# Counting the edges of a graph network beside two of its edge sums, in place of a stage of their own

## What is computed

```python
# layer 0: a small network on every edge, summed at its target
out = segment_sum(leaky(norm(leaky(norm([x[src], x[dst]] @ w1)) @ w2)) * edge_weight, dst)
# layer 1, twice: mean over the incoming edges
mean = segment_sum(h[src], dst) / maximum(segment_sum(1, dst), 1)
# layer 2, twice: the edges and a loop at each node, scaled by the root of the count on both sides
deg  = segment_sum(1, dst) + 1
out  = segment_sum((x @ W)[src] / sqrt(deg[src] * deg[dst]), dst) + b
# layer 3: softmax over the edges that leave a node, then a weighted sum at dst
```

## Time and profile before

| | us |
|---|---|
| median of 3 runs | 8127.6 |
| lowest and highest | 8127.11, 8133.38 |
| the profiled execution | 8135.82 |
| its span, first to last instruction | 8134.1 |

### The profile page before, as it was taken

How to read it: one execution, slowest core, us unless ns; L and a number is a source line. 1 busy time by engine, 2 the same in 40 slices (tenths; PEclk the granted TensorE clock), 3 DMA queues, 4 the chain that set the end, 5 groups by cost and what they waited for, 6 DMA issues and landing times. The chain is left out here.

```text
span 8134.1 us, 136717 instructions
## 1 busy us (share of the span) xinstructions
PE 5193.6 (64%) x26951; PEld 4126.4 (51%) x26952; DVE 4104.8 (50%) x13878; ACT 2865.5 (35%) x7066; POOL 4035.8 (50%) x4542
## 2 busy tenths in 40 slices
PE   4446766666037696669767857666666666605667
PEld 1125555555036585558656646544444444404555
DVE  8965555533522321236523422386566666653568
ACT  0015555523623431258524313573111111100249
POOL 0037777500057504770277167504777777707740
PEclk7767777788556897589857966897777777755689
DMA  0002222255633484349646745674222222232458
GB/s 3 0 23 72 73 73 73 68 177 195 203 102 101 138 247 135 93 124 312 227 116 189 244 124 152 194 259 139 65 68 68 68 65 68 64 25 69 105 164 298
DMA packets 616678, 1013.31 MB, mean 125 GB/s; under 512 B 174962, under 2 KB 177296, under 8 KB 616336
## 3 DMA queue, kind: packets, MB, share of 16 engines
q1 hardware_dynamic: 279472, 417.77, 17.6%
q10 hardware_dynamic: 211680, 385.45, 13.3%
q0 software_dynamic: 125440, 209.18, 10.9%
HBM read 648.88 MB, written 363.07 MB: 124 GB/s over the span
## 5 line engine op out<-in xcount | busy, mean ns | idle before, releaser
L397 PE MATMUL agg_bank<-agg_msgs,agg_onehot 128*128 x7840 | 1620.5, 374 | 894.0 <-DVE agg_onehot L372 695.9
L397 PEld LDWEIGHTS agg_bank<-agg_msgs,agg_onehot 128*128 128x128 f32 x7840 | 1403.7, 268 | 1114.1 <-issue 1104.6
L372 DVE TENSOR_TENSOR agg_onehot<-iota,rel 128x512 f32<-128x512 f32 x1176 | 814.3, 692 | 1819.4 <-PE agg_bank L397 856.5
L303 POOL DMA_INDIRECT agg_msgs<-y,agg_rows x784 | 776.6, 991 | 234.8 <-issue 189.9
L291 POOL COPY agg_rows<-src_row_of 128x16 int32 (+2 forms) x100 | 23.5, 235 | 1623.4 <-POOLq L59 1623.1
L397 PE MATMUL agg_bank<-agg_weighted,agg_onehot 128*128 x1568 | 339.9, 387 | 217.1 <-DVE agg_onehot L372 168.6
L1090 POOL DMA_INDIRECT mlp_xs<-in_x,mlp_rows x392 | 412.4, 1052 | 120.1 <-issue 119.2
L300 POOL DMA_INDIRECT agg_weight<-weights,agg_rows x392 | 409.7, 1045 | 123.3 <-issue 99.6
L424 ACT ACTIVATE agg_kept<-agg_bank,inv_root 128x128 f32<-128x128 f32 x784 | 224.1, 368 | 700.3 <-PE agg_bank L397 679.7
L424 ACT ACTIVATE agg_kept<-agg_bank,inv_deg 128x128 f32<-128x128 f32 x784 | 224.1, 368 | 695.4 <-PE agg_bank L397 694.7
L1422 PE MATMUL score_pSrc<-ident,score_xs 128*128 128x128 f32 x392 | 154.3, 401 | 485.2 <-issue 356.2
(11 more groups left out here) (338 smaller groups left out, 12993.9 us busy)
## 6 DMA issues: line engine op xcount, KB each, us to landing
sums<-agg_kept ACTq DMA_DIRECT2D x588, 256.0 KB
agg_first<-y ACTq DMA_DIRECT2D x196, 256.0 KB
messages<-mlp_m SPq DMA_DIRECT2D x98, 256.0 KB, 2.1
agg_first<-in_x ACTq DMA_DIRECT2D x98, 256.0 KB
agg_msgs<-messages SPq DMA_DIRECT2D x98, 256.0 KB
l_z<-sums SPq DMA_DIRECT2D x98, 256.0 KB
x<-l_o ACTq DMA_DIRECT2D x98, 256.0 KB
l1a_s<-sums SPq DMA_DIRECT2D x98, 256.0 KB
```

The lines of the kernel that those rows point to most:

```text
L303: pool.indirect_dma_start(msgs[:, j, :], None, table[:, :], bass.IndirectOffsetOnAxis(ap=rows[:, third, j:j + 1], axis=0)).then_inc(sm[f"g ...
L372: nc.vector.tensor_tensor(onehot[:, j, :, :], k.iota[:, 0:P].unsqueeze(1).to_broadcast([P, Q, P]), k.rel[:, ds(i * (4 * Q) + j * Q, Q)].un ...
L397: t.matmul(bank[:, column[q], :], onehot[:, j, q, :], messages[:, slot[q], :], start=False, stop=True, skip_group_check=True)\
```

## The change

The stage `count_nodes` is gone. The splits of `src` and `dst` into tile and place go to `setup`, for both. `aggregate` gets an argument `tally`. In `agg0` it holds the split of `dst`, in `agg3` that of `src`. There each round of four steps also takes two edge tiles: VectorE makes two pairs of hot rows behind `onehot`, TensorE does two matmuls into a bank of counts behind the reading of the places, with the semaphores `hot` and `tallied` between them and four buffers. 196 rounds of two tiles are the 392. What was worked out from the counts now stands at the end of these two sums. The other four sums are as before but for more names of semaphores to clear.

```diff
+                for to_lo, to_hi, node in ((k.src_lo, k.src_hi, k.src_i), (k.dst_lo, k.dst_hi, k.dst_i)):
+                    c.link(v.tensor_scalar(part_i[:, :], node[:, :], P - 1, None, ALU.bitwise_and))
+                    c.link(v.tensor_copy(to_lo[:, :], part_i[:, :]))
+                    c.link(v.tensor_scalar(part_i[:, :], node[:, :], 7, None, ALU.logical_shift_right))
+                    c.link(v.tensor_copy(to_hi[:, :], part_i[:, :]))
+                c.link(v.memset(k.zero_row[:, :], 0.0))
...
                             ALU.is_equal).then_inc(sm["onehot"], 1)
+                        if tally is not None:
+                            dve.wait_ge(sm["tallied"], i * 4 + (j + 1))
+                            for w in range(2):
+                                at = i * 8 + (j * 2 + w)
+                                nc.vector.tensor_scalar(hot_lo[:, j, w, :], k.iota[:, 0:P], tally[0][:, ds(at, 1)], None, ALU.is_equal)
+                                last = nc.vector.tensor_scalar(hot_hi[:, j, w, :], k.iota[:, 0:NT], tally[1][:, ds(at, 1)], None, ALU.is_equal)
+                            last.then_inc(sm["hot"], 1)
+
+                v, c = nc.vector, Chain(dve, sm["tally_c"])
+
+                def count_in():
+                    c.link(v.tensor_scalar(k.inv_deg[:, :], counts[:, 0:NT], 1.0, None, ALU.max))
+                    c.link(v.tensor_scalar(k.inv_root[:, :], counts[:, 0:NT], 1.0, None, ALU.add))
+                    dve.sem_inc(sm["tally_to_act"], 1)
+                    c.link(v.reciprocal(k.inv_deg[:, :], k.inv_deg[:, :]))
+                    dve.wait_ge(sm["tally_rooted"], 1)
+                    c.link(v.reciprocal(k.inv_root[:, :], k.root[:, :]))
...
+                if tally is not None:
+                    dve.wait_ge(sm["tallied"], STEPS // Q + 4)
+                    if tally[0] is k.dst_lo:
+                        count_in()
+                    else:
+                        count_out()
...
+                if tally is not None:
+                    t.matmul(counts[:, 0:NT], k.zero_row[0:1, 0:P], k.zero_row[0:1, :], start=True, stop=True)
+                    pe.sem_inc(sm["tallied"], 4)
                 pe.sem_inc(sm["summed"], SHIFT)
...
                             pe.reg_load(regs[half:half + Q], k.places[0:1, ds(i * 4 + (j + 1), 1), half:half + Q])
+                        if tally is not None:
+                            pe.wait_ge(sm["hot"], i * 4 + (j + 1))
+                            for w in range(2):
+                                last = t.matmul(counts[:, 0:NT], hot_lo[:, j, w, :], hot_hi[:, j, w, :], start=False, stop=True, skip_group_check=True)
+                            last.then_inc(sm["tallied"], 1)
+                if tally is not None and tally[0] is not k.dst_lo:
+                    pe.wait_ge(sm["tally_to_pe"], 1)
+                    t.matmul(off[:, 0:1], below[:, :], scan[:, NT - 1:NT], start=True, stop=True).then_inc(sm["tally_offset"], 1)
...
+                if tally is not None and tally[0] is k.dst_lo:
+                    act.wait_ge(sm["tally_to_act"], 1)
+                    a.activation(k.root[:, :], k.inv_root[:, :], ACT.Sqrt).then_inc(sm["tally_rooted"], 1)
...
-        count_nodes(nc, k)
...
-        aggregate(nc, k, "agg0", messages, None, sums, before=ins["x"])
+        aggregate(nc, k, "agg0", messages, None, sums, before=ins["x"], tally=(k.dst_lo, k.dst_hi))
...
-        aggregate(nc, k, "agg3", y2, k.src_row, sums, before=y2, scale=k.inv_root)
+        aggregate(nc, k, "agg3", y2, k.src_row, sums, before=y2, scale=k.inv_root, tally=(k.src_lo, k.src_hi))
```

More of the change, by code:

```diff
@@ L244, in setup, with aggregate @@
         end_phase(nc, sm)
-def aggregate(nc, k, name, table, rows_of_edges, out, before=None, scale=None, weights=None):
+def aggregate(nc, k, name, table, rows_of_edges, out, before=None, scale=None, tally=None, weights=None):
     BLOCKS, REST = ET // RING, ET % RING
@@ L257, in aggregate @@
     sm = phase(nc, name, [f"gathered{j}" for j in range(loads)] + [f"written{u}" for u in range(BANKS)] + [f"before{u}" for u in range(BANKS)]
-               + [f"weight{u}" for u in range(RING // Q)] + ["rows", "pass_pool", "pass_dve", "arrived", "onehot", "summed", "zeros", "cleared", "ready", "emptied", "weighted"])
+               + [f"weight{u}" for u in range(RING // Q)] + ["rows", "pass_pool", "pass_dve", "arrived", "hot", "tallied", "tally_c", "tally_to_act", "tally_rooted", "tally_to_pe", "tally_offset", "onehot", "summed", "zeros", "cleared", "ready", "emptied", "weighted"])
     with ExitStack() as ctx:
@@ L265, in aggregate @@
         kept = sb("kept", [P, BANKS, Q, C])
+        if tally is not None:
+            hot_lo, hot_hi = sb("hot_lo", [P, 4, 2, P], BF16), sb("hot_hi", [P, 4, 2, NT], BF16)
+            counts = ctx.enter_context(nc.psum_tensor(name + "_counts", [P, 512], F32))
+            scan, one_row, below, offset = sb("scan", [P, NT]), sb("one_row", [P, NT]), sb("below", [P, P]), sb("offset", [P, 1])
+            off = ctx.enter_context(nc.psum_tensor(name + "_off", [P, 512], F32))
         if rows_of_edges is not None:
@@ L376, in _, with count_out @@
                             ALU.is_equal).then_inc(sm["onehot"], 1)
+                        if tally is not None:
[13 more added lines that the diff above has]
+                    c.link(v.reciprocal(k.inv_root[:, :], k.root[:, :]))
+                def count_out():
+                    c.link(v.memset(one_row[:, :], 1.0))
+                    c.link(v.tensor_scalar(below[:, :], k.iota[:, 0:P], k.pid[:, 0:1], None, ALU.is_gt))
+                    c.link(v.tensor_tensor_scan(scan[:, :], one_row[:, :], counts[:, 0:NT], 0.0, ALU.mult, ALU.add))
+                    dve.sem_inc(sm["tally_to_pe"], 1)
+                    c.link(v.tensor_tensor(k.first_place[:, :], scan[:, :], counts[:, 0:NT], ALU.subtract))
+                    dve.wait_ge(sm["tally_offset"], 1)
+                    c.link(v.tensor_copy(offset[:, :], off[:, 0:1]))
+                    c.link(v.tensor_scalar(k.first_place[:, :], k.first_place[:, :], offset[:, 0:1], None, ALU.add))
+                if tally is not None:
[4 more added lines that the diff above has]
+                        count_out()
             @block.tensor
@@ L1767, in allocate @@
     k.src_hi = sb("src_hi", [P, ET])
+    k.dst_lo = sb("dst_lo", [P, ET])
+    k.dst_hi = sb("dst_hi", [P, ET])
+    k.zero_row = sb("zero_row", [1, NT], BF16)
     k.src_row = sb("src_row_of", [P, ET], I32)
```

79 lines of the change are left out of this document (removed).

## The result

| | before | changed |
|---|---|---|
| median of the runs shown together, us | 8128.98 (4 runs) | 7720.11 (4 runs) |
| lowest and highest | 8127.11, 8133.38 | 7718.73, 7721.56 |
| the profiled execution | 8135.82 | 7720.17 |
| mean granted clock | 0.74 | 0.76 |

The changed kernel takes 0.9497 of the time, 95% interval 0.9485 to 0.9509: 408.9 us less. The forecast was 7766, with 7710 to 7834 around it. The sign and the range held, but the likeliest value was 46 us too high, and 7720 lies 10 us from the first rival's 7710, near the low end of the range. So the question is which term of the sum went wrong.

What follows compares the result with a forecast made beforehand. Stages add up; TensorE's queue was taken to bound the first sum, POOL's gathers most of the fourth. -432.1 + 3.5 + 39 + 16 + 7 + 4.3 + 0.5 = -361.8 us, giving 7766 us, range 7710 to 7834.

Steps and rivals of the forecast that it cites:

- first rival: Both sums: clock stays fast and the new matmuls sit in TensorE's 0.7 us idle gap each round; 7710 us, 20% chance.
- Stage removed, setup longer: Counting stage and its barrier go, -432.1 us; eight conversions and a memset move into setup, +3.5 us.
- VectorE in the first sum: Two hot-row pairs add 1.06 us a round, 1.8 to 1.9 in all, under TensorE's 2.08: no cost.
- TensorE in the first sum: Point 4 of the prediction: one more wait and two matmuls a round lengthen the first sum by 39 us.
- With 62% of the time fast: First sum: old clock mix kept, rounds of 2.15 us fast and 2.54 slow give a mean of 2.28.
- One more wait: First sum: a further wait in TensorE's queue, read from the sixth sum, adds 0.11 us a round.
- TensorE in the fourth sum: Same addition to TensorE's rounds, but only the last 105 or so are near its limit: +16 us.
- POOL in the fourth sum: Gathers beside VectorE's new operations slow by 0.032 us each, 12.5 us, less 5 where TensorE is the limit: +7.
- Ends: After the last matmul, the work on the counts adds 4.3 us to the first sum and 0.5 to the fourth.
- The issue is dear: Both sums: each new matmul holds TensorE's queue 0.15 us, +80 for +39 and +43 for +16; 7834 us, 17% chance.
- POOL is locked out: Fourth sum: each of 392 gathers waits for a full hot-row pair, 0.53 us, +208 for +7; 7967 us, 4% chance.
- Lock-step: Both sums: VectorE and TensorE wait for each other, 4.3 us a round, +764; 8475 us, slower than before, 2% chance.

Runs made afterwards that it cites:

- e2: Changed kernel, but the first sum's hot rows are zeroed once and not made, its two matmuls a round kept: 8847.7 us, ratio 0.9529; first sum 410.6 us.
- e10: Changed kernel, unedited, rerun on another chip: 8860.1 us beside 9278.1 for the kernel before, ratio 0.9559; first sum 411.8 us, fourth 619.4.
- e5: Changed kernel, but both counts in the first sum (four hot-row pairs and matmuls a round), none in the fourth: 8958.0 us, ratio 0.9629; first sum 530.0 us.
- e1: Changed kernel, but the first sum's count matmuls left out, hot rows and waits kept: 8872.1 us, ratio 0.9548; first sum 431.8 us.
- e11: Repeat, on another chip, of the changed kernel without the first sum's count matmuls, hot rows and waits kept: 8848.1 us, ratio 0.9557; first sum 432.3 us.
- e12: Changed kernel, but the first sum has neither hot rows nor count matmuls, only the waits and increments: 8864.8 us, ratio 0.9567; first sum 430.4 us.
- e8: Changed kernel with the source count moved to the fifth sum; fourth sum does two matmuls a round on zeroed rows, no hot rows: 8856.2 us, fourth sum 605.9.
- e7: Changed kernel with the source count moved to the fifth sum; fourth sum makes hot rows without matmuls, waits kept: 8886.3 us, fourth sum 617.4.
- e6: Changed kernel, but outgoing edges counted beside the fifth sum, not the fourth: 8849.2 us, ratio 0.9523; fourth sum 601.7 us, fifth 617.9.
- e9: Kernel before the change, unedited, rerun on another chip: 9283.5 us, ratio 1.0; first sum 406.9 us, fourth 603.7.

## Why the prediction was right, and where it was not

1. **Stage removed, setup longer: right.** -428.3 for -428.6, and -427.4 on another chip.
2. **VectorE in the first sum: right.** 1.06 us a round and no cost while VectorE is ahead; e2 without the hot rows is within 1.2 us of e10, and e5 shows the 0.53 a pair at full load. The 1.8 to 1.9 that it took for VectorE's round was a little high, as e5's distances make it 0.6 + 2 x 0.53 = 1.66.
3. **TensorE in the first sum: wrong, and 34 of the 46 us.** Forecast +39, measured +4.7, which is the prediction's own sign of being wrong, a first sum within 10 us of its old length. Two steps of the prediction's fourth point failed.
   - "With 62% of the time fast" took the granted clock of before as given. The change itself set it: 3 slow rounds in place of 69, and with the matmuls a clock of 0.99 (e2, e10), without them 0.76 to 0.78 (e1, e11, e12), whatever VectorE does. The 2.54 us for a slow round was about right. The first sum has too few of them left to tell (2.42 for three, 2.73 for two in e10), but the slow rounds of the fourth sum, shown under e10, take 2.52 and 2.36 where they wait for nothing. With every round at the forecast's fast 2.15 the term would have been 196 x (2.15 - 2.08) = 14, so by this estimate 25 of the 34 us missed are the clock.
   - "One more wait", +0.11. It was read from the sixth sum, where no run separates it. e12 gives 0.11 to 0.12 for a wait and an increment together that have nothing to ride on. In the changed kernel they are part of the count's matmuls and cost nothing that can be seen. This is the other 9 us.
4. **TensorE in the fourth sum: wrong.** Forecast +16; e8, the matmuls without the hot rows, gives +4.2, and the ledger leaves nothing for it. From TensorE's starts the last 105 rounds took 225.9 us before and take 230.4, 4.5 more with POOL's part in them. The clock was taken as given here too: in these rounds it went from 0.82 to 0.99.
5. **POOL in the fourth sum: right in kind, and too small by the deduction.** 32 ns a gather was taken from the scatters of the scoring stage, and the gathers grew by 32 ns on the first chip: 12.5 us. That it is the same number is luck, since they grew by 22 ns in e10 and 14 in e7. I had let 5 of them go as hidden under TensorE's limit, and since TensorE didn't become the limit, they weren't.
6. **Ends: right.** +4.1 for +4.3, and -0.8 for +0.5.

The range held because it reached down to the first rival, not because the forecast's mechanism was right. *TensorE hides it* is what happened, and it deserved more than its 20%. What I held against it, that the clock fell before with the array just as busy, was an argument from a kernel without the matmuls. *The issue is dear* falls: four matmuls cost 1.9 us and eight 16.1, all of it array. *POOL is locked out* falls by the fourth sum's 12.2 us, and by e7. *Lock-step* falls: both sums together grew by 17 us and not by 764.

What stays open: why the array's clock went up. Shown is that it goes up with the matmuls and down without them; what of their activity matters was not separated. Nor do the runs tell why the standing semaphores cost 0.11 at the fast clock and 0.15 at the slow one. I found no version that beats the change: both counts in the first sum are slower (e5), and the fifth sum is no cheaper than the fourth (e6). The dense stages between the sums, which have no gathers, were not tried as a place; in each of them VectorE or TensorE is busy for over half of the time.

## What to carry to other kernels

Work for an engine that a queue bounds was nearly free here as long as its matmuls fitted into the gap and brought no standing wait or increment into that queue: let both ride on the work. Don't carry the granted clock of the old profile into the sum: added matmuls can set it, so work out a fast and a slow case and name which the change makes likelier. And a neighbour's price read from another stage of the same kernel, here 32 ns a gather, was of the right size, where the worst case, a wait for every pair, was some 200 us off.

## What the runs showed of the hardware that I had not expected

- **More matmuls, and the higher clock.** Two matmuls of 392 columns in each round's gap took the first sum's granted clock from 0.81 to 0.98, that of the fourth from 0.66 to 0.82. In the first sum zeros do as well as data (e2); without the matmuls it has 0.76 to 0.78.
- **Semaphores without an instruction cost more than two matmuls.** e12 loses 23.5 us against before for a wait and an increment a round; the changed kernel, which has these riding on its 392 matmuls, loses 4.9 (e10).
- **Chips on which all engines stop together.** On the three chips of the experiments before takes 9278 to 9294 us and not 8129. In the stages with POOL's DMAs there are times at which no engine starts anything: in e9's profile 535 times over 1 us, 809 us in all, against 116 times and 232 us in that of the first chip. That is 577 us of the 1152 by which the one profile is longer; in the fourth sum they are few (16 us in e9), and what makes that sum longer is that POOL sits idle between gathers: 38 times over 1.5 us, 100 us in all, where it never does on the first chip. One stop of all engines, from e6's timeline in the fourth sum:

```profile
4101.85 1.29 POOL L316 DMA_INDIRECT agg_msgs<-y,agg_rows  x1 [0.30 <-issue]
...
4102.24 0.76 PE L447 MATMUL agg_bank<-agg_msgs,agg_onehot 128*128 x2 [1.25 <-issue]
...
4103.14 0.21 POOL L304 COPY agg_rows<-src_row_of 128x16 int32 x1
...
4105.21 1.14 ACT L482 ACTIVATE agg_kept<-agg_bank,inv_root 128x128 f32<-128x128 f32 x4 [16.34 <-DMA messages<-mlp_m]
...
4105.30 0.69 DVE L385 TENSOR_TENSOR agg_onehot<-iota,rel 128x512 f32<-128x512 f32 x1 [2.97 <-DMA messages<-mlp_m]
...
4105.44 1.86 PE L447 MATMUL agg_bank<-agg_msgs,agg_onehot 128*128 x7 [2.44 <-issue]
...
4105.97 0.97 POOL L316 DMA_INDIRECT agg_msgs<-y,agg_rows  x1 [2.62 <-DMA messages<-mlp_m]
```

TensorE issues two of a round's passes at 4102.24 and the others from 4105.44 on, with "issue" as the cause, though VectorE had waited for that round's messages before it made the one-hot; ACT, VectorE and POOL start again within the same 0.8 us. The gathers before and after take 1.29 and 0.97 us, where the mean is 0.99. The cause is not in the profile.
